# Leaving PSUM in two plain copies: sorting values and softmax sums by twelve small DMAs

## The reference, cut to what matters

```
att = softmax(einsum('bthd,bshd->bhts', q, k), axis=-1)
o = einsum('bhts,bshd->bthd', att, v).reshape(B, T, D)
return o @ out_w.T + out_b
```

## Time and profile before

| | |
|---|---|
| three runs | 1794.47, 1795.82, 1800.01 us |
| median | 1795.82 us |
| span of the profiled execution | 1797.6 us |
| time of the profiled execution beside its span | none is given; the span is 1.8 us above the median |
| `attend` | from about 247 us to 1649 us of the span |
| one slot in the steady part | 26.4 to 27.1 us |
| granted TensorE clock, mean of the span | 0.934 |

### The profile page before, as it was taken

One profiled execution on the slowest core, in us unless ns is written; L12 is line 12 of the kernel. 1 busy time (PEld: TensorE's weight loads), 2 busy tenths in 40 slices (PEclk: granted clock), 3 DMA queues, 4 the chain that ended last, 5 costly groups with the idle time before them and its releaser, 6 DMA issues. The chain is left out here.

```text
span 1797.6 us, 37140 instructions
## 1 busy us (share of the span) xinstructions
PE 1598.6 (89%) x9686; PEld 738.5 (41%) x9686; DVE 1274.2 (71%) x3085; ACT 1217.8 (68%) x2393; POOL 697.2 (39%) x673
## 2 busy tenths in 40 slices
PE   4659946889999999999999999999999999955998
PEld 1217932334444444434444344444444443211665
DVE  5986856388787877878787787878787787352442
ACT  3325741757888878788878878787887878714333
POOL 7822441234344344344334334434434433221442
PEclk9768955989999999999999999999999999857999
DMA  2211125354565455465456456446545635030122
GB/s 51 74 43 37 47 47 71 43 80 60 65 77 66 64 71 79 54 75 74 57 70 77 67 61 79 62 60 76 70 63 69 81 52 65 2 36 26 57 61 59
DMA packets 131811, 108.99 MB, mean 61 GB/s; under 512 B 21809, under 2 KB 124721, under 8 KB 131761
## 3 DMA queue, kind: packets, MB, share of 16 engines
q1 hardware_dynamic: 129712, 104.18, 41.5%
q0 software_dynamic: 2048, 4.20, 0.9%
HBM read 20.05 MB, written 8.39 MB: 16 GB/s over the span
## 5 line engine op out<-in xcount | busy, mean ns | idle before, releaser
L1000 ACT ACTIVATE probs<-psum 128x512 f32<-128x512 f32 (+3 forms) x1536 | 739.6, 551 | 262.4 <-PE psum L1111 159.7
L888 DVE TENSOR_REDUCE mx_S<-psum 128x1 f32<-128x512 f32 x512 | 323.1, 682 | 77.0 <-PE psum L1096 76.5
L888 DVE TENSOR_REDUCE mx_C<-psum 128x1 f32<-128x512 f32 x512 | 319.0, 682 | 56.8 <-PE psum L1096 55.2
L888 DVE TENSOR_REDUCE mx_T<-psum 128x1 f32<-128x128 f32 (+3 forms) x512 | 240.4, 488 | 120.7 <-PE psum L1099 109.5
L824 POOL TENSOR_TENSOR rem_q<-f_q,parts_q 128x512 f32<-128x512 f32 x48 | 55.5, 1155 | 496.9 <-ACT parts_q L986 480.0
L1096 PE MATMUL psum<-ks_S,qs_S 96*128 96x512 bf16 x512 | 201.7, 400 | 26.4 <-DMA ks_S<-parts_k 21.8
L1096 PE MATMUL psum<-ks_C,qs_C 96*128 96x512 bf16 x512 | 202.7, 397 | 12.5 <-DMA ks_C<-parts_k 7.4
L1111 PE MATMUL psum<-qs_C,ks_C 99*128 99x512 bf16 x512 | 194.7, 392 | 18.0 <-ACT probs L1000 10.7
L1111 PE MATMUL psum<-qs_S,ks_S 99*128 99x512 bf16 x512 | 196.0, 384 | 1.6 <-ACT probs L1000 0.9
L1096 PE MATMUL psum<-ks_T,qs_T 96*128 96x128 bf16 (+3 forms) x512 | 157.5, 310 | 7.1 <-DMA ks_T<-parts_k 6.0
L1111 PE MATMUL psum<-qs_T,ks_T 99*128 99x256 bf16 (+3 forms) x512 | 153.3, 302 | 2.5 <-ACT probs L1000 1.7
(11 more groups left out here) (184 smaller groups left out, 2732.5 us busy)
## 6 DMA issues: line engine op xcount, KB each, us to landing
qs_S<-parts_q SPq DMA_DIRECT2D x96, 128.0 KB, 4.5
ks_S<-parts_k SPq DMA_DIRECT2D x96, 128.0 KB, 7.0
qs_T<-parts_q SPq DMA_DIRECT2D x96, 128.0 KB, 4.4
ks_T<-parts_k SPq DMA_DIRECT2D x96, 128.0 KB, 7.0
qs_C<-parts_q SPq DMA_DIRECT2D x96, 128.0 KB, 4.5
ks_C<-parts_k SPq DMA_DIRECT2D x96, 128.0 KB, 6.9
w_in_S<-in_s_in SPq DMA_DIRECT2D x16, 257.0 KB, 2.7
w_in_T<-in_t_in SPq DMA_DIRECT2D x16, 257.0 KB, 2.7
```

The lines of the kernel that those rows point to most:

```text
L888: nc.vector.tensor_reduce(mx[kind][:, n:n + 1], psum[:, ring_place(kind, b, n, RL), 0:last_key], AX_X, ALU.max)\
L1000: nc.scalar.activation(probs[:, n // 4 % 2, n % 4, t0:T], psum[:, LOGITS + ring_place(kind, b, n, RC), t0:T], ACT.Exp, scale=SCALE).then_i ...
```

## The change

The scaled copies, the columns `low` and `high`, the two POOL additions and the DVE shuffle are removed. ACT makes one plain copy of the whole bank at step 28 (`group_0`) and one at step 12 (`group_1`). Twelve DMAs of 32 KB (16 partitions of 2 KB each) sort the halves: four put the sums of group 0 into `s_all`, four those of group 1, and four put the values of group 1 into the halves of `group_0` that are free by then. SP issues eight of them (`gather_1`) between the query stack and the key stack of the slot, and four (`gather_0`) behind the key stack. Ln reads `s_all` and waits for the landing of the first eight; the multiplication on POOL waits for the last four.

```diff
+                def halves(to, to_at, source, at, done):
+
+                    for j in range(4):
+                        sp.dma_start(to[32 * j + to_at:32 * j + to_at + HD, :],
+                                     source[32 * j + at:32 * j + at + HD, :]).then_inc(done, 16)
+
+                def gather_0(kind, b):
+                    u = unit_no(kind, b)
+                    sp.wait_ge(low_out, u + 1)
+                    halves(s_all, 0, group_0, HD, sums_0_in)
+
+                def gather_1(kind, b):
+                    u = unit_no(kind, b)
+                    sp.wait_ge(high_out, u + 1)
+                    halves(s_all, HD, group_1, 0, sums_1_in)
+                    sp.wait_ge(sums_0_in, 64 * u + 64)
+                    halves(group_0, HD, group_1, HD, values_1_in)
...
-                    stack(kn, bn)
+                    stack(kn, bn, 0)
+                    if exists(bo):
+                        gather_1(ko, bo)
+                    stack(kn, bn, 1)
+                    if exists(bb):
+                        gather_0(kb, bb)
...
-                    if exists(bo):
-                        u = unit_no(ko, bo)
-                        pool.wait_ge(high_out, u + 1)
-                        pool.wait_ge(low_out, u + 1)
-                        nc.gpsimd.tensor_tensor(s_all[:], s_all[:], s_high[:], ALU.add).then_inc(s_merged, 1)
-                        nc.gpsimd.tensor_tensor(u_all[:], u_all[:], u_high[:], ALU.add).then_inc(u_merged, 1)
...
-                        pool.wait_ge(u_merged, u + 1)
+                        pool.wait_ge(values_1_in, 64 * u + 64)
...
-                        nc.gpsimd.tensor_tensor(oT[:], u_all[:], s_recip[:], ALU.mult).then_inc(o_ready, 1)
+                        nc.gpsimd.tensor_tensor(oT[:], group_0[:], s_recip[:], ALU.mult).then_inc(o_ready, 1)
...
-                def swap(kind, b):
-
-                    u = unit_no(kind, b)
-                    dve.wait_ge(s_merged, u + 1)
-                    at_least(dve, logged, u)
-                    settle(nc, scrap)
-                    nc.vector.stream_shuffle(s_right[:], s_all[:], mask=list(range(HD, 32)) + list(range(HD)))\
-                        .then_inc(swapped, 1)
...
-                    at_least(act, u_merged, u)
-                    nc.scalar.activation(s_high[:], sums, ACT.Copy, scale=low[:])
-                    nc.scalar.activation(u_high[:], sums, ACT.Copy, scale=high[:]).then_inc(high_out, 1)
+                    at_least(act, sums_1_in, 64 * u)
+                    at_least(act, values_1_in, 64 * u)
+                    nc.scalar.activation(group_1[:], sums, ACT.Copy).then_inc(high_out, 1)
...
-                    act.wait_ge(swapped, u + 1)
-                    nc.scalar.activation(s_log[:], s_right[:], ACT.Ln).then_inc(logged, 1)
+                    act.wait_ge(sums_0_in, 64 * u + 64)
+                    act.wait_ge(sums_1_in, 64 * u + 64)
+                    nc.scalar.activation(s_log[:], s_all[:], ACT.Ln).then_inc(logged, 1)
...
-                            at_least(act, swapped, u)
-                            nc.scalar.activation(s_all[:], sums, ACT.Copy, scale=high[:])
                             at_least(act, o_ready, u)
-                            nc.scalar.activation(u_all[:], sums, ACT.Copy, scale=low[:]).then_inc(low_out, 1)
+                            nc.scalar.activation(group_0[:], sums, ACT.Copy).then_inc(low_out, 1)
```

More of the change, by code:

```diff
@@ L39 @@
 GROUP_1_AT, GROUP_2_AT = 28, 12
-SWAP_AT, RECIP_AT = 17, 21
+RECIP_AT = 21
 OUTPUT_AT, KEEP_AT = 29, 31
@@ L117, in program @@
         ident = ctx.enter_context(nc.sbuf_tensor("ident", [P, P], F32))
-        low = ctx.enter_context(nc.sbuf_tensor("low", [P, 1], F32))
-        high = ctx.enter_context(nc.sbuf_tensor("high", [P, 1], F32))
         eps_t = ctx.enter_context(nc.sbuf_tensor("eps_t", [P, NB], F32))
@@ L127, in program @@
         scrap = ctx.enter_context(nc.sbuf_tensor("scrap", [1, 1], F32))
-        shared = (scrap, ident, low, high, eps_t, minus_half, norm_cols, expert, X, xhatT, psum)
+        shared = (scrap, ident, eps_t, minus_half, norm_cols, expert, X, xhatT, psum)
         embed_and_mix(nc, shared, x_ids, table, w12, router_w1, router_b1, router_w2, router_b2, norms, out_v)
@@ L161, in embed_and_mix @@
 def embed_and_mix(nc, shared, x_ids, table, w12, router_w1, router_b1, router_w2, router_b2, norms, out_v):
-    scrap, ident, low, high, eps_t, minus_half, norm_cols, expert, X, xhatT, psum = shared
+    scrap, ident, eps_t, minus_half, norm_cols, expert, X, xhatT, psum = shared
     with ExitStack() as ctx:
@@ L214, in embed_and_mix @@
         consts = sem("consts")
-        halves = sem("halves")
         got = [sem("got0"), sem("got1")]
@@ L363, in _ @@
                 dve.wait_ge(consts, 2)
[L365 to L368, removed]
                 def negate(half):
@@ L669, in attend @@
         probs = sb("probs2", [P, 2, 4, T])
-        u_all = sb("u_all", [P, T])
+        group_0 = sb("group_0", [P, T])
+        group_1 = sb("group_1", [P, T])
         s_all = sb("s_all", [P, T])
-        u_high = sb("u_high", [P, T])
-        s_high = sb("s_high", [P, T])
-        s_right = sb("s_right", [P, T])
         s_log = sb("s_log", [P, T])
@@ L699, in attend @@
         high_out = sem("high_out")
-        s_merged, u_merged = sem("s_merged"), sem("u_merged")
-        swapped = sem("swapped")
+        sums_0_in, sums_1_in, values_1_in = sem("sums_0_in"), sem("sums_1_in"), sem("values_1_in")
         logged = sem("logged")
@@ L770, in weights, with stack @@
                     sp.dma_start(tile[:], packs[bass.ds(e, 1), :, :].rearrange("o p n -> p (o n)")).then_inc(done, 16)
-                def stack(kind, b):
+                def stack(kind, b, c):
                     if exists(b):
-                        if not isinstance(b, int) or b >= 1:
+                        if c == 0 and (not isinstance(b, int) or b >= 1):
                             sp.wait_ge(logits_in, TILES * (unit_no(kind, b - 1) + 1))
[L776 to L781, removed]
+                        tile, order = ((qs[kind], Q_PARTS), (ks[kind], K_PARTS))[c]
+                        sp.wait_ge(lo_done, 2 * unit_no(kind, b) + c + 1)
+                        sp.wait_ge(mid_done, 2 * unit_no(kind, b) + c + 1)
+                        for g in range(NPROD):
+                            sp.dma_start(tile[HD * g:HD * g + HD, :, :],
+                                         parts[c][:, order[g], :]).then_inc(stack_in[kind], 16)
@@ L783, in slot_program @@
                 def slot_program(i, slot):
-                    (kn, bn), _, (kb, bb), _ = units(i, slot)
+                    (kn, bn), _, (kb, bb), (ko, bo) = units(i, slot)
                     if exists(bb):
@@ L801, in _ @@
                     sp.dma_start(tile[:], source).then_inc(w_fixed, 16)
-                stack("S", 0)
+                stack("S", 0, 0)
+                stack("S", 0, 1)
                 whole_loop(sp, slot_program)
@@ L944, in slot_program @@
                         if exists(bo):
-                            if n == SWAP_AT:
-                                swap(ko, bo)
                             if n == KEEP_AT and ko == "T":
```

## The result

The changed kernel takes 1979.05 us (median of 4 runs, 1974.6 to 1979.9) against 1797.7 us for the kernel before: ratio 1.100, 95% interval [1.0988, 1.1019]. The span of its profiled execution is 1978.1 us. It is slower, as forecast, and inside the range (1922 to 2088). The change costs (1979.1 - 1797.7 - 3) / 46 = 3.9 us a slot.

The account below looks back on a forecast made before the run. PE sets the pace, with the stack's landing and ACT's step 21 almost as critical. Stalls of 138 us, half clock of 110 and the last unit's 3 sum to 251 on 1795.8: 2045 us, range 1922 to 2088.

Parts of the forecast that it names:

- The stack's 0.2 us: At a slot's first score: the twelve stacking DMAs of queries and keys land 0.2 us before PE needs them.
- step 21's 0.1 us of slack: On ACT at step 21: more than about 0.1 us later makes PE stand still at step 24.
- Removed work is worth 0 to 19 us: Fewer copies on ACT, additions on POOL, shuffles on DVE: taken as 0, range 0 to -19 us.
- Eight issues, 5.1 us, keys' landing 8.9 us after the first: On SP, `gather_1` delays the keys' issue; the slot's first score starts 3.0 us later.
- Ln's wait, 2.9 us, passing whole to PE: At step 21 ACT waits 2.9 us for the sums' DMAs; PE stands still as long, less 0.1, at step 24.
- rival C: Small DMAs slip through and keys land fast: 0.6 to 1.6 us a slot, 1825 to 1870 us; chance 0.08.
- The two don't add: Ln's stall and the keys' delay hold PE in the same slot: 3.0 us per slot once, 46 x 3.0 = 138 us.
- Half clock, 2.4 us a slot: PE's clock falls to 0.50 after the stall in eight slots of ten: 46 x 2.4 = 110 us.
- The last unit, 3 us: At the end, with no cover, DMA issues and landing of 7.0 us replace 4.1 us of work: 3 us more.
- B: Rival: the same stall, but the clock holds at 1.00: 46 x 3.0 + 3, 1925 to 1945 us; chance 0.21.
- A: The forecast itself, stall and falling clock: 46 x 4.4 to 46 x 6.2, 2000 to 2085 us; chance 0.60.
- D: Rival: SP issues the eight small DMAs in 0.27 us each and Ln's wait vanishes: about 1777 us; chance 0.02.

Follow-up runs that it names:

- dummy8: The kernel before with eight more 32 KB DMAs, which nobody waits for until the end, between the query six and the key six: 1959.5 us, ratio 1.091.
- wait7: The kernel before, with Ln at step 21 also waiting for the seventh of the slot's twelve stacking DMAs: 2000.2 us, ratio 1.113.
- no_gather1: The changed kernel without the eight DMAs between the sixes and their waits, second group's sums and values left out: 1793.6 us, ratio 0.9969.
- wait5: The kernel before, with Ln at step 21 also waiting for the slot's fifth stacking DMA: 1831.0 us, ratio 1.0186.
- filler: The changed kernel with three more fp32 matmuls on PE at step 24, result unread: 1923.5 us, ratio 1.0707 to the kernel before.
- wait6: The kernel before, with Ln at step 21 also waiting for the slot's sixth stacking DMA: 1921.3 us, ratio 1.0672.
- pool_queue: The changed kernel with the second group's eight DMAs on GpSimd's queue, Ln at step 25, output at step 30: 2087.1 us, ratio 1.1606.

## Why the prediction was right, and what was mis-sized

- **What bounds.** Right. The stack's 0.2 us and step 21's 0.1 us of slack were the decisive readings: dummy8 and wait7 each remove one of them, and each costs 9 to 11%.
- **Removed work is worth 0 to 19 us.** Right: 4 us (no_gather1), where the sum took 0. That a relieved PE meets the keys sooner is shown there.
- **Eight issues, 5.1 us, keys' landing 8.9 us after the first.** Right in mechanism: 5.25 and 8.4. So the keys' path costs 2.6 us a slot (dummy8), not 3.0.
- **Ln's wait, 2.9 us, passing whole to PE.** Right: 3.0 us per wait, PE 3.07 in the slot shown; wait5 shows it one for one. The stall of 1.1 us, an estimate by the fit of the Trainium skill ("DMA: Bandwidth & Descriptors", section "Anatomy of one DMA — SWDGE (gpsimd) path"), was left to rival C. The fit's 2.1 us for 32 KB agrees with the trace where nothing is ahead: the four DMAs issued from 992.11 us land after 1.9 to 2.0 us. Behind the queries the sums landed 3.9 to 5.0 us after their issues.
- **The two don't add.** Right: filler runs at clock 1.00 with both in place and costs 126 us, or (126 - 3) / 46 = 2.7 us a slot, where the term said 3.0. 138 us became 123.
- **Half clock, 2.4 us a slot.** Right that it falls, wrong in size: 56 / 46 = 1.2 us. Of the 66 us that the forecast was too high, 54 are this term and 15 the one before (2 go the other way, from the median of before, 1797.7 and not 1795.8). The term was a fall in eight slots of ten, at 3.0 us each; the share was too low and the price too high. In windows of 1 us the clock falls in all 42 slots between 404 and 1665 us, so one fall costs 56 / 42 = 1.3 us, an estimate. wait6 gives 1.4 (above), and dummy8 1.3: it has 33 falls there, and 162 - 46 x 2.6 = 42 us beyond the keys' delay.

  I had taken 6.0 us of half clock from the one stall in the trace of before; in the slot shown it is 3.4 us, from 987.5 to 990.9, and PE is back at 1.00. So it is in 38 of the 42 falls; four have 6.8 us, one of them after a stall of 3.03 us that ended at 893.97:

```profile
895.30:902.10 6.80, 6.80 (x29) 3.09 (x26) 3.45 (x7) 3.94 (x8) 2.04 (x3) 0.50 0.67 80
```

  Half of 3.4 us is 1.7 us of PE's work, and about 1.3 us of it shows in the time. What makes one fall longer than another was not tried.
- **The last unit, 3 us.** From its first copy of step 12 to `oT` it is 7.0 us (1818.94 to 1825.98) where it was 4.9 (1641.40 to 1646.32): 2.1 us more.
- **The rivals.** B, the clock holds, is what filler builds: it forecast 1925 to 1945 and filler gives 1923.5. The measured time lies between B and A: both stalls and the falling clock are A's mechanism, at a smaller price. The range held it because it took in both. C and D needed landings or issues that no run showed.

## What to carry to other kernels

Before moving work to DMAs, look at what the issuing queue does at that moment: here an SBUF-to-SBUF issue took 0.64 us of SP's time, at 32 KB as at 128 KB, all that stood behind it moved by as much, and DMAs of 32 KB behind six of 128 KB landed after 3.9 to 5.0 us instead of 2. An engine with a low busy share is no measure of what relieving it brings; the wait that ends last at each hand-over is. And a stall of TensorE in dense work can cost more than its length, so look at the granted clock behind it: here the half clock added 1.2 us a slot on top of 2.7, while a stall of 0.8 us (wait5) cost its own length.

## What the runs showed of the hardware that I had not expected

- A stall of 0.8 us per slot left the granted clock at 1.00, one of about 1.9 us brought the mean to 0.95, one of 3 us to 0.94, with 3.4 us at 0.50 after it in the slot shown and 6.8 us in another.
- Matmuls without use, put into a stall, made the kernel 2.8% faster (1979.1 to 1923.5 us).
- An SBUF-to-SBUF DMA issued by GpSimd took 0.49 us of its time, less than SP's 0.59 us for one of the same size.
- DMAs of 32 KB on GpSimd's queue landed in 1.8 to 1.9 us with nothing else under way, and in 6.1 to 8.4 us while six of 128 KB on SP's queue were (pool_queue).
